# Half of the mask loads issued from ScalarE, and the second normalisation run chunk by chunk, in an eight-core masked-linear plus LoRA-FFN kernel

## The reference

```
x = x + layernorm(masked_linear(layernorm(x)))      # masked_linear: w = weight * block_mask, + bias
x = x + layernorm(ffn(layernorm(x)))

block_mask: mask (4096 x 4096, int32) summed over 32 x 32 blocks, > 0
ffn(h) = h @ W_up.T + LoRA of the expert that argmax(h @ gate_w.T + expert_bias) picks
         (4 experts, rank 8)
x: 1 x 8192 x 4096 float32, weight and W_up 4096 x 4096
```

## Time and profile before

| | before |
|---|---|
| median of three runs | 1655.8 us |
| profiled execution, its time | 1654.27 us |
| profiled execution, its span (slowest core, core 0) | 1652.7 us |
| PE busy in the span | 1105.1 us, 67% |
| DVE busy | 602.2 us, 36% |
| ACT busy | 355.6 us, 22% |
| mean granted TensorE clock, core 0 | 0.887 |

### The profile page before, as it was taken

One profiled execution on the slowest core, in us unless ns is written; L12 is line 12 of the kernel. 1 busy time (PEld: TensorE's weight loads), 2 busy tenths in 40 slices (PEclk: granted clock), 3 DMA queues, 4 the chain that ended last, 5 costly groups with the idle time before them and its releaser, 6 DMA issues.

```text
span 1652.7 us, 25827 instructions; the slowest of 8 cores (1640.9 to 1652.7 us)
## 1 busy us (share of the span) xinstructions
PE 1105.1 (67%) x9240; PEld 868.3 (53%) x9240; DVE 602.2 (36%) x861; ACT 355.6 (22%) x1185; POOL 79.5 (5%) x96
## 2 busy tenths in 40 slices
PE   0211249898998988989331222799999999999600
PEld 0100137676776776767210111677777777777500
DVE  1565765556546555553635444100000000000680
ACT  1211212122221222222333323122222222222200
POOL 1000000000000000000000000000000000000241
PEclk9999999999999999999655555899999999999855
DMA  8922225767778676661643425044234324423399
GB/s 183 331 79 88 43 64 130 187 177 181 179 181 192 169 192 174 165 156 57 173 184 140 164 104 150 4 74 81 52 55 78 74 52 76 79 52 59 117 293 346
DMA packets 39996, 220.40 MB, mean 133 GB/s; under 512 B 4850, under 2 KB 4866, under 8 KB 21442
## 3 DMA queue, kind: packets, MB, share of 16 engines
q0 software_dynamic: 11792, 84.46, 26.1%
q1 hardware_dynamic: 23330, 100.74, 18.3%
q10 hardware_dynamic: 4752, 33.56, 5.6%
HBM read 252.86 MB, written 33.55 MB: 173 GB/s over the span
## 4 chain that ended last, share of the span: by engine, by line
PE 51%; DVE 19%; DMA 16%; issue 9%; ACT 2%; DVEq 1%; ACTq 0%; POOLq 0%; POOL 0%; SPq 0%
PE pm L379 42%; DMA mring<-mw 12%; PE pt L215 5%; DVE psj_i L306 3%; DVE wmb L350 2%; DVE sums_h L258 2%; PE pm L393 2%; DVE xbst L273 1%; DMA mo<-x 1%; DMA y<-wmb 1%; DVE mo L542 1%; ACT junk L524 1%; DVE cmp L566 1%; DVEq L691 1%; PE pm L386 1%
## 5 line engine op out<-in xcount | busy, mean ns | idle before, releaser
L379 PE MATMUL pm<-wmb,fm 128*128 128x256 bf16 x8192 | 950.6, 275 | 38.3
L379 PEld LDWEIGHTS pm<-wmb,fm 128*128 128x128 bf16 x8192 | 790.3, 98 | 175.9 <-issue 80.0
L399 ACT ACTIVATE mo<-pm 128x256 bf16<-128x256 f32 x256 | 98.3, 384 | 791.9 <-PE pm L386 415.6
L306 DVE TENSOR_REDUCE psj_i<-mring 128x32 int32<-128x1024 int32 x128 | 156.2, 1220 | 218.6 <-DMA mring<-mw 213.0
L215 PE MATMUL pt<-identb,xbst 128*128 128x128 bf16 x288 | 44.9, 288 | 225.6 <-DVE xbst L273 187.2
L186 DVE TENSOR_REDUCE st_d<-acc_s 128x1 f32<-128x16 f32 x8 | 1.4, 170 | 489.1 <-ACT junk L407 488.4
L215 PEld LDWEIGHTS pt<-identb,xbst 128*128 128x128 bf16 x288 | 24.8, 115 | 245.8 <-issue 239.5
L350 DVE TENSOR_TENSOR wmb<-wmb,bmpj 128x4096 bf16<-128x4096 bf16 x32 | 141.6, 4425 | 11.0 <-DMA wmb<-bw 7.9
L407 ACT ACTIVATE junk<-pm 128x256 bf16<-128x256 f32 x256 | 98.3, 384 | 23.5
L215 PE MATMUL pt<-identb,mo 128*128 128x128 bf16 x224 | 39.6, 288 | 92.2 <-DVE mo L542 83.8
L215 PEld LDWEIGHTS pt<-identb,mo 128*128 128x128 bf16 x224 | 19.3, 115 | 112.6 <-issue 112.0
(11 more groups left out here) (120 smaller groups left out, 420.1 us busy)
## 6 DMA issues: line engine op xcount, KB each, us to landing
mring<-mw SPq DMA_DIRECT2D x128, 512.0 KB, 5.1
wmb<-bw POOLq DMA_DIRECT2D x32, 1024.0 KB, 10.1
wmb<-bu POOLq DMA_DIRECT2D x32, 1024.0 KB, 7.8
mo<-x POOLq DMA_DIRECT2D x12, 1024.0 KB, 24.6
wmb<-x SPq DMA_DIRECT2D x8, 1024.0 KB, 7.1
xst<-x SPq DMA_DIRECT2D x8, 1024.0 KB, 6.6
xmid<-wmb ACTq DMA_DIRECT2D x8, 1024.0 KB, 4.7
xmid<-xst ACTq DMA_DIRECT2D x8, 1024.0 KB, 4.6
```

The costliest lines, as they stand in the source:

```text
L306: return e.tensor_reduce(out=psj_i32[:, (j % 2) * 256 + pc * 32:(j % 2) * 256 + (pc + 1) * 32], in_=mring[idx % 2][:, :].rearrange("p (g w ...
L379: return e.matmul(bank[0:128, 0:NS], fm[:, k * 1024 + i * 128:k * 1024 + i * 128 + 128], wmb[wpar][:, k * NS:(k + 1) * NS], start=(k == 0) ...
L399: return e.activation(out=mo[:, i * 4096 + j * NS:i * 4096 + (j + 1) * NS], in_=bank[0:128, 0:NS], func=AF.Identity, accum_out=acc_s[:, i ...
```

## The change

Two things are changed. The load of a mask piece with an odd index goes from the queue of SyncE (SP) into the stream of ScalarE; its waits stay as they were. In phase 4 stages A and B of a chunk stand together in one loop body, with no stage A of the next chunk between, and the slot pairs are handed out otherwise: chunks 0, 2 and 4 use the halves of `wmb0`, chunks 1, 3, 5, 6 and 7 all use the two `xst` buffers, so that chunk 6 waits for chunk 5 and chunk 7 for chunk 6. The first load into `wmb0` in phase 5 waits for the last chunk that used it, which is now chunk 4 and was chunk 6.

```
-                t_d = E("sync", fd, waits=[seg_tok.get(((idx - 2) // 8, (idx - 2) % 8))],
+                t_d = E("sync" if idx % 2 == 0 else "scalar", fd,
+                        waits=[seg_tok.get(((idx - 2) // 8, (idx - 2) % 8))],
                         inc="dM%d" % (idx % 2), amt=16)
...
-        pmap4 = [i % 2 for i in range(TC)]
+        pmap4 = [(i % 2) if i < TC - 2 else 1 for i in range(TC)]
...
-        prev_same4 = {i: (i - 2 if i >= 2 else None) for i in range(TC)}
-
-        def p4_stageA(i):
+        prev_same4 = {}
+        lastu = {}
+        for i in range(TC):
+            prev_same4[i] = lastu.get(pmap4[i])
+            lastu[pmap4[i]] = i
+        for i in range(TC):
             pr = pmap4[i]
...
-                    waits=[trh[h], apply4_tok.get(i - 2)], inc="sA")
+                    waits=[trh[h], apply4_tok.get(prev_same4[i])], inc="sA")
...
-            return slots, hts
-
-        def p4_stageB(i, slots, hts):
-            pr2 = i % 2
-            t_r3, t_q3 = stats_chain("c" if pr2 == 0 else "d",
+            t_r3, t_q3 = stats_chain("c" if pr == 0 else "d",
...
-        ctxs = {}
-        for i in range(TC):
-            ctxs[i] = p4_stageA(i)
-            if i >= 1:
-                p4_stageB(i - 1, *ctxs[i - 1])
-        p4_stageB(TC - 1, *ctxs[TC - 1])
```

More of the change, by code:

```diff
@@ L488, in build_program @@
         sq4_tok = {}
-        pmap4 = [i % 2 for i in range(TC)]
+        pmap4 = [(i % 2) if i < TC - 2 else 1 for i in range(TC)]
+        if TC >= 2:
+            pmap4[0] = 0
         pairs4 = [w0slots, xslots]
-        prev_same4 = {i: (i - 2 if i >= 2 else None) for i in range(TC)}
-        def p4_stageA(i):
+        prev_same4 = {}
[4 more added lines that the diff above has]
+        for i in range(TC):
             pr = pmap4[i]
@@ L513, in p4_stageA @@
             for h in range(2):
-                sl = (i % 2) * 2 + h
+                sl = pr * 2 + h
                 def fr(e, i=i, h=h, ap_slot=slots[h][0], sl=sl):
@@ L530, in p4_stageA @@
             sq4_tok[i] = hts[1][1]
-            return slots, hts
-        def p4_stageB(i, slots, hts):
-            pr2 = i % 2
-            t_r3, t_q3 = stats_chain("c" if pr2 == 0 else "d",
-                                     hts[1][0], hts[1][1], sl=(pr2 * 2, pr2 * 2 + 1),
-                                     r_ap=rqP4[:, pr2 * 2:pr2 * 2 + 1],
-                                     q_ap=rqP4[:, pr2 * 2 + 1:pr2 * 2 + 2])
+            t_r3, t_q3 = stats_chain("c" if pr == 0 else "d",
+                                     hts[1][0], hts[1][1], sl=(pr * 2, pr * 2 + 1),
+                                     r_ap=rqP4[:, pr * 2:pr * 2 + 1],
+                                     q_ap=rqP4[:, pr * 2 + 1:pr * 2 + 2])
             xb4 = xbst if i == 0 else mo[:, (i - 1) * 4096:i * 4096]
@@ L541, in p4_stageB @@
             for h in range(2):
-                ap = E("vector", lambda e, h=h, pr2=pr2, xb4=xb4, ap_slot=slots[h][0]: e.tensor_scalar(
+                ap = E("vector", lambda e, h=h, pr=pr, xb4=xb4, ap_slot=slots[h][0]: e.tensor_scalar(
                     out=xb4[:, h * HALF:(h + 1) * HALF], in0=ap_slot,
-                    scalar1=rqP4[:, pr2 * 2:pr2 * 2 + 1],
-                    scalar2=rqP4[:, pr2 * 2 + 1:pr2 * 2 + 2],
+                    scalar1=rqP4[:, pr * 2:pr * 2 + 1],
+                    scalar2=rqP4[:, pr * 2 + 1:pr * 2 + 2],
                     op0=ALU.mult, op1=ALU.add),
```

## The result

| | before | changed |
|---|---|---|
| median | 1655.3 us (8 runs) | 1870.2 us (8 runs, 1866.4 to 1873.0) |
| ratio, 95% interval | | 1.1297, 1.1281 to 1.1312 |
| span of the slowest core in the profile | 1652.7 us | 1869.8 us |
| PE busy | 1105.1 us | 1125.0 us |
| mean granted TensorE clock, slowest core | 0.887 | 0.846 |

What follows compares the result with a forecast made beforehand. PE and DVE's mask chain run neck and neck in the attention stages; phase 4 is a serial chain. Stages 1 to 13 +169.8, stage 14 -2.1, phase 4 +8: +176, 1832 us on the median, range 1770 to 1872.

Steps and rivals of the forecast that it cites:

- the likeliest case: Whole kernel: the forecast itself, +176 us, 1832 on the median, chance 0.62, own range 1800 to 1858.
- the rival of long landings: Stages 1 to 13: sharing queues lands piece 1, at worst also piece 3, 1.7 us later; up to 1876 us; chance 0.17.
- The hold of ACT's evictions by load 7: Stages 1 to 13: load 7 waits for piece 5's reduction, PE idles 14.3 us after four groups; 13.05 more a stage.
- Stage 0 spared: Stage 0: stage 1's weights are already in, so the hold costs only 0.2 us, left out.
- Stage 14 gaining 2.1: Stage 14: PE did not wait before it, so its first group takes 3.65 us, not 5.73; -2.1.
- The landing of piece 1, 9.28: Stages 1 to 13: piece 1, issued at 1.15 behind the last eviction, takes 9.28 us and lands at 10.4.
- The landing of piece 3, 8.69: Stages 1 to 13: piece 3, issued at 11.85 after piece 1 is reduced, takes 8.69 us and lands at 20.5.
- The restart, 1.65: Stages 1 to 13: PE's first group after its idle stretch takes 5.30 us instead of 3.65, 1.65 more.
- Phase 4, +8: Phase 4: chunk by chunk, losing overlap, takes 243.4 us against 235.3; bounds +4 to +14.
- The rival of short landings: Stages 1 to 13: landings of 4.56 us each, stage 39.65, +61, 1717 us; chance 0.16 for short or partly short.
- Faster: Attention stages: ACT's loads do not hold up the evictions; 1626 us, at half the gain 1645; chance 0.03.

Runs made afterwards that it cites:

- one-queue kernel: Kernel before, all mask loads on SP, two added waits holding each attention stage's first eviction and piece 1 of each stripe: 1834.5 us, ratio 1.1108.
- mask part alone: Kernel before with only the odd mask loads moved to ACT, phase 4 as before: 1856.8 us, ratio 1.1228.
- small weight loads: Changed kernel with attention weights of stripes 2 to 14 loaded only in the first 128 columns of each half: 1703.5 us, ratio 1.0301.
- piece 1 on SP: Kernel before with mask pieces 3, 5 and 7 on ACT ahead of the evictions, piece 1 staying on SP: 1778.2 us, ratio 1.0752.
- ACT loads where due: Kernel before with odd mask loads on ACT, placed among the evictions so none is issued later than DVE frees its buffer: ratio 1.0023.
- stage A in the gap: Kernel before with phase 4's next-chunk additions put behind this chunk's apply, its store and squares behind the copies: 1613.7 us, ratio 0.9757.

## Why the prediction was right, and where it was short

The forecast was +176 on 1655.8, the time came out at +215: 1870.2, under the upper end of the range by 1.8 us and above the likeliest case's own range, whose end was 1858. The mechanism held and its size was short by a fifth. The number alone would fit the rival of long landings, whose worst case was 1876 us; but that rival's own term, the sharing of two queues, makes 17 of the 39 to 41 us that are missing, and the rest comes from terms of the forecast itself.

- **The hold of ACT's evictions by load 7**: right. PE stood after the fourth group in each of stages 1 to 13, and the stage began without a gap. Holding the evictions without any load on ACT shows it (49.63 apart), taking a bank away shows it (54.90), and moving the loads takes it away (36.05).
- **Stage 0 spared**: true of the sum, by luck. Stage 1 begins at 270.74, against 270.90, but PE did stand in stage 0, before its fifth group, and restarted at the lower clock; I had left out 0.2 us there:

```profile
253.02 5.32 PE L380 MATMUL pm<-wmb,fm 128*128 128x256 bf16 x32 [1.80 <-ACT junk L408]
```

From its first group to the small matmul stage 0 took 36.6 us instead of 34.0, and it began 2.8 us earlier, which no term of the forecast gave. The other cores stood 0.4 to 1.9 us there.
- **Stage 14 gaining 2.1**: the last two stages took 2.2 less.
- **The landing of piece 1, 9.28**: the term that was mis-sized most. It measured 10.96, 1.7 more in each of 13 stages, 22 us. I took a duration that Rows 3 show for a load issued at t = 2.4 and gave it to one issued at 1.15. But the first of these loads lands about 1 us behind the weight half beside it, whether it was issued at 1.2 or at 2.4: at t = 11.7 in the kernel before, at 11.4 with one queue and the holds, at 12.2 in the changed one, with the weight half at 10.5, 10.6 and 10.7 (over the eight cores 10.7, 10.6 and 11.4). That the end stays and the duration grows was 0.9 of it, by the one-queue kernel; the rest is the sharing of two queues, the rival that I put at 1.7 for piece 1 and again for piece 3, and that measured 1.0 and 0.3 in the mask part alone. The rule on queues that take turns (the Trainium skill, DMA: Bandwidth & Descriptors, Queues, rings and completion order) thus pointed the right way, at 1.3 of the 3.4 us given to it.
- **The landing of piece 3, 8.69**: measured 8.73. That this one is right and piece 1 carries the whole error is the chance of the slowest core; on cores 1, 3, 4 and 6 piece 1 took 9.6 to 9.8 and piece 3 10.1 to 10.4. What was short is the sum of the two, 17.97 forecast and 19.6 to 20.0 measured on every core.
- **The restart, 1.65**: the group after PE's idle stretch took 6.05 on average of 13, not 5.30, 0.75 more a stage, 10 us. I took it from the 5.30 of one row; the first groups of late stages before ran from 4.89 to 5.87, and in the changed kernel the other cores' means are 5.4 to 6.1, 5.74 over all eight. Such groups scatter more than they differ by how long PE stood: 4.98 to 6.50, mean 5.6, after 4 to 5 us (small weight loads); 4.93 to 6.54, mean 5.6, after 9 to 12 (piece 1 on SP); 4.92 to 6.55, mean 5.8, after 16 to 18 (mask part alone). What sets the scatter is open.
- **Small gaps** between the links (DVE to a load, DVE to ACT and back), which is what the other terms leave: 0.5 more a stage, 7 us.
- **Phase 4, +8**: +10.6. From first addition to reciprocal it was 9.47 on average against 9.32, the rest of a chunk 21.3 against 21.15. The loads of chunks 6 and 7 were hidden, as said.

The terms give 22 + 0.5 + 10 + 7 + 2.6 = 42 more, against the 41 by which +217 lies above +176. Over the eight cores a stage took 51.29, 2.84 above the 48.45 of the forecast: 1.87 by the sum of the two landings, 0.44 by the restart, 0.53 by the gaps. The rival of short landings fell: on the slowest core of the changed kernel none was under 7.9 us at pieces 1 and 3. Faster was out of reach, since even with both landings under 4 us the hold remained.

The rule that DMAs issued from several engines only save issue time (the Trainium skill, DMA: Bandwidth & Descriptors, Issuing engines are not separate DMA queues) agrees with the kernel whose ACT loads stand where due, 1.0023.

## What to carry to other kernels

A DMA issue put on an engine that does arithmetic brings its wait along: ask what stands behind it on that engine and how many buffers the producer upstream has until then, here four groups of 4 us against a wait of 31. When loads are late for a consumer, look first at how many may be in flight: two more ring buffers in memory that lay idle took 2.6% off, a second queue nothing. And in a serial chain, put the next item's work into a wait of the same engine rather than ahead of it or behind it.

## What was not expected of the hardware

A load of 512 KB issued beside one of a weight half (1024 KB written) did not take its own time from its issue: the first one landed on average 0.8 to 1.4 us behind the weight half, 11 to 12 us after that one's issue, be it issued 0.7 or 1.9 us after it; with the small weight loads pieces 1 and 3 took 3.4 to 4.4. How long it took depended on the neighbouring core as well, as said above. And an idle stretch of 1.96 us was followed by a group that began at half the granted clock and took 5.30 us, about the price after 18 us (5.14 in stage 1); but not every short one is: stretches of 2.80 us (ACT loads where due, stage 3) and 2.84 (stage A in the gap, stage 10) left the clock at 1.00 and the group at 3.65.
